# One graph layer with a gated unit in front of a plain graph layer: four queues put in another order, and the last subtraction of the blend given to TensorE

## The reference, cut to what matters

```
h = relu(layernorm(x))
conv = relu(bn2(conv1d_17(relu(bn1(conv1d_1(h.T))))) + h.T).T   # 17 taps along the nodes
s = h @ w_se.T + b_se                                            # 3 coordinates a node
A = exp(-|s_n - s_m|^2) * adj
nmp = A @ relu(h @ w_msg.T + b_msg)
r, z = sigmoid(gates of [conv, nmp] and h);  c = tanh(i_n + r * h_n)
x = x + (1 - z) * c + z * h
h2 = relu(layernorm(x))
x = x + adj @ (h2 @ weight) + bias
```

## Time and profile before

| | |
|---|---|
| median of 3 runs | 334.1 us (333.93 to 334.57) |
| the profiled execution | 334.82 us |
| its span, first to last instruction | 333.0 us |
| granted TensorE clock, mean | 1.000 |
| PE busy | 322.2 us, 97% of the span |
| PEld busy | 290.7 us, 87% |
| DVE busy | 259.7 us, 78% |
| ACT busy | 224.1 us, 67% |
| POOL busy | 145.3 us, 44% |

### The profile page before, as it was taken

One profiled execution on the slowest core, in us unless ns is written; L12 is line 12 of the kernel. 1 busy time (PEld: TensorE's weight loads), 2 busy tenths in 40 slices (PEclk: granted clock), 3 DMA queues, 4 the chain that ended last, 5 costly groups with the idle time before them and its releaser, 6 DMA issues.

```text
span 333.0 us, 6260 instructions
## 1 busy us (share of the span) xinstructions
PE 322.2 (97%) x2162; PEld 290.7 (87%) x2162; DVE 259.7 (78%) x746; ACT 224.1 (67%) x434; POOL 145.3 (44%) x128
## 2 busy tenths in 40 slices
PE   8799999989999999999999999999999999989995
PEld 5588787879889997899989998899989998889894
DVE  5788999899679977799679977789678766772475
ACT  2899668778668767687758776696767745443353
POOL 7130352139701793129801694119901594127014
PEclk9999999999999999999999999999999999999999
DMA  7902000002200131002300131001200010000003
GB/s 240 341 15 94 1 2 0 3 0 89 102 2 3 33 126 33 0 1 66 126 2 0 34 105 54 0 0 67 65 0 0 2 47 18 1 2 0 3 0 127
DMA packets 7951, 15.02 MB, mean 45 GB/s; under 512 B 1008, under 2 KB 1648, under 8 KB 7792
## 3 DMA queue, kind: packets, MB, share of 16 engines
q1 hardware_dynamic: 7776, 14.62, 12.9%
q10 hardware_dynamic: 144, 0.01, 0.0%
HBM read 10.43 MB, written 4.19 MB: 44 GB/s over the span
## 4 chain that ended last, share of the span: by engine, by line
issue 44%; POOL 30%; PE 11%; DVE 8%; ACT 4%; DMA 1%; POOLq 1%; DVEq 0%
POOL rs L1424 5%; POOL rs L1419 3%; POOL x_ring L1461 3%; POOL px L1010 3%; POOL px L1020 3%; POOL ac L1016 2%; POOL px L1013 2%; POOL base L1478 2%; POOL base L1469 2%; POOL base L1467 2%; POOL base L1475 2%; ACT hn L719 2%; DVE st L1033 1%; DMA x_ring<-x_in 1%; PE pP L328 1%
## 5 line engine op out<-in xcount | busy, mean ns | idle before, releaser
L1424 POOL TENSOR_TENSOR rs<-ve,neg_half 128x4 f32<-128x4 f32 x15 | 18.7, 1249 | 132.1 <-DVE ve L1192 132.1
L327 PE MATMUL pP<-cx_hi,conv_hi 128*128 128x256 f32 (+1 forms) x179 | 53.7, 300 | 0.0
L329 PE MATMUL pP<-cx_hi,conv_lo 128*128 128x256 f32 (+1 forms) x179 | 51.4, 287 | 0.0
L328 PE MATMUL pP<-cx_lo,conv_hi 128*128 128x256 f32 (+1 forms) x179 | 51.4, 287 | 0.0
L327 PE MATMUL pQ<-cx_hi,conv_hi 128*128 128x256 f32 (+1 forms) x139 | 41.6, 299 | 2.0 <-DVE cx_lo L1116 1.2
L329 PE MATMUL pQ<-cx_hi,conv_lo 128*128 128x256 f32 (+1 forms) x139 | 39.7, 285 | 0.0
L328 PE MATMUL pQ<-cx_lo,conv_hi 128*128 128x256 f32 (+1 forms) x139 | 39.6, 285 | 0.0
L327 PEld LDWEIGHTS pP<-cx_hi,conv_hi 128*128 128x128 f32 x179 | 33.9, 190 | 0.5
L328 PEld LDWEIGHTS pP<-cx_lo,conv_hi 128*128 128x128 f32 x179 | 33.8, 189 | 0.5
L329 PEld LDWEIGHTS pP<-cx_hi,conv_lo 128*128 128x128 f32 x179 | 33.7, 188 | 0.4
L327 PEld LDWEIGHTS pQ<-cx_hi,conv_hi 128*128 128x128 f32 x139 | 26.2, 189 | 2.6 <-issue 2.4
(11 more groups left out here) (281 smaller groups left out, 967.6 us busy)
## 6 DMA issues: line engine op xcount, KB each, us to landing
x_ring<-x_in SPq DMA_DIRECT2D x16, 256.0 KB, 2.8
adj_ring<-adj_in SPq DMA_DIRECT2D x16, 256.0 KB, 3.0
out<-x_ring SPq DMA_DIRECT2D x15, 256.0 KB, 2.0
work<-conv_in SPq DMA_DIRECT2D x1, 1088.0 KB, 7.7
x_ring<-gate_in SPq DMA_DIRECT2D x1, 576.0 KB, 8.3
out<-x_ring SPq DMA_DIRECT2D x2, 128.0 KB, 1.8
early<-early_in SPq DMA_DIRECT2D x1, 129.5 KB, 3.8
late<-late_in SPq DMA_DIRECT2D x1, 128.0 KB, 8.4
```

The source lines that it names most:

```text
L327: pe.matmul(acc, w_hi, m_hi, start=start, stop=False)
L328: pe.matmul(acc, w_hi, m_lo, start=False, stop=False)
L329: return pe.matmul(acc, w_lo, m_hi, start=False, stop=stop)
L1424: pool.tensor_tensor(rs2[g % 2][:], ve2[g % 2][:], neg_half[:, 0:GG], ALU.pow).then_inc(rs2_set, 1)
```

## The change

1. SP loads x of group 0 in two transfers of two graphs each, on a semaphore each; DVE's statistics of graphs 0 and 1 wait for the first, those of 2 and 3 for the second.
2. The order on ACT in the opening: `place_bias(0)` comes between `hidden_hi(0)` and `hidden_hi(1)`; `round_w(0)` ahead of `conv1_out(0)`; `hidden_graphs(0)` behind `conv1_out(1)`; `hidden_copy(0)` behind `split_hi_first(0)`; later `hidden_graphs(2)` ahead of `decay(0)`. On DVE `split_w(0)` comes ahead of `sum_odd` and `less_odd`.
3. The order on DVE in step 1: both `split_lo(1, 3)` and `split_lo(1, 4)` move back, `coordinates(4)` and `right_rows(4)` forward. In step 7, `between(7)` comes ahead of `shift2(13)`.
4. The blend of group 15: DVE no longer subtracts. PE multiplies `zh` by the identity (`last_turn_kept`) and adds `cand` times the negated identity to it (`last_turn_less`), in the same bank. POOL makes `neg_ident` once, in the opening.
5. PE in `ending()`: the three groups of `keep_clock` (2, 4 and 3 matmuls) go; `layer2(12)` and `layer2(13)` come behind the last turn; `end_pass(0)` comes ahead of `layer2(14)`. ACT makes the first half of group 15's h2 ahead of `turned_up(14)`. POOL does `with_bias(14)` ahead of `scale2_half(0)`, once DVE has made the last `cand`.

```diff
-            load_x(0)
+            sp.dma_start(two(xs(0), 0), two(x_in[:, 0:W], 0)).then_inc(x_first, 16)
+            sp.dma_start(two(xs(0), 1), two(x_in[:, 0:W], 1)).then_inc(x_loaded[0], 16)
...
+            def last_turn_kept():
+                have(pe, zh_set, END + 1)
+                have(pe, v_set, END + 1)
+                for j in range(GG):
+                    pe.matmul(graph(pI, j), lane(zh[END % 2], j), ident[:], start=j == 0, stop=True, skip_group_check=True)
+
+            def last_turn_less():
+                have(pe, zn_set, END + 1)
+                pe.wait_ge(neg_set, 1)
+                for j in range(GG):
+                    last = pe.matmul(graph(pI, j), lane(cand[END % 2], j), neg_ident[:], start=False, stop=True,
+                                     skip_group_check=True)
+                last.then_inc(o_placed, 1)
...
-                keep_clock(2)
+                last_turn_kept()
+                last_turn_less()
                 layer2(END - 3)
-                keep_clock(4)
-                o_turn(END)
                 layer2(END - 2)
                 adj_h2(END - 1)
+                end_pass(0)
                 layer2(END - 1)
-                keep_clock(3)
-                end_pass(0)
                 end_pass(1)
...
                 hidden_hi(0)
+                place_bias(0)
                 hidden_hi(1)
-                place_bias(0)
-                hidden_copy(0)
-                hidden_graphs(0)
+                act.wait_ge(conv_loaded, 16)
+                round_w(0)
                 conv1_out(0)
                 conv1_out(1)
-                act.wait_ge(conv_loaded, 16)
-                round_w(0)
+                hidden_graphs(0)
                 split_hi_first(0)
+                hidden_copy(0)
                 hidden_copy(1)
                 hidden_graphs(1)
                 round_w(1)
...
                 first(3)
+                hidden_graphs(2)
                 decay(0)
                 left_rows(1)
-                hidden_graphs(2)
...
                 second(END - 1)
-                turned_up(END - 1)
                 have(act, l1_done, END - 1)
                 for j in range(GG):
+                    if j == 2:
+                        turned_up(END - 1)
...
                 blend_start(qq)
+                shift2(pp)
                 if t == 1:
-                    split_lo(1, 3)
-                shift2(pp)
+                    coordinates(a)
                 blend_end(qq)
...
                     right_rows(a)
+                    if t == 1:
+                        split_lo(1, 3)
                     pairs(b)
+                    if t == 1:
+                        split_lo(1, 4)
+                if middle and not front:
+                    between(t)
                 shift2(qq)
...
                 blend_start(END)
                 shift2(p)
-                blend_end(END)
+                scaled_candidate(END)
                 residual(END)
...
+                pool.tensor_scalar(neg_ident[:], ident[:], -1.0, None, ALU.mult).then_inc(neg_set, 1)
...
                 scale2(END - 1)
+                pool.wait_ge(zn_set, END + 1)
+                with_bias(END - 1)
                 scale2_half(0)
```

More of the change, by code:

```diff
@@ L69, in gnn_kernel @@
         ident = sb("ident", [128, 128])
+        neg_ident = sb("neg_ident", [128, 128])
         warm = sb("warm", [128, 1])
@@ L152, in gnn_kernel @@
             sem, ("st1_set", "mv1_set", "ve1_set", "rs1_set", "nb1_set", "hn_set"))
-        hn_half = sem("hn_half")
+        hn_half, x_first, neg_set = sem("hn_half"), sem("x_first"), sem("neg_set")
         hT_placed, hhi_set, hG_set, hT_set, hlo_set = map(sem, ("hT_placed", "hhi_set", "hG_set", "hT_set", "hlo_set"))
@@ L1029, in normalise1 @@
                 lane = slice(lanes[0][2], lanes[-1][2] + 1)
-                for g in groups:
-                    dve.wait_ge(x_loaded[g % XRING], 16 * (g // XRING + 1))
+                if groups[0]:
+                    for g in groups:
+                        dve.wait_ge(x_loaded[g % XRING], 16 * (g // XRING + 1))
+                else:
+                    dve.wait_ge(x_first, 16)
                 for g, j, i in lanes:
+                    if (g, j) == (0, 2):
+                        dve.wait_ge(x_loaded[0], 16)
                     last = dve.bn_stats(st1[:, i, :], xs(g, j))
@@ L1165, in blend_start, with scaled_candidate, blend_end @@
                 dve.scalar_tensor_tensor(zh[g % 2], tz, 1.0, half(hT, g), ALU.add, ALU.mult).then_inc(zh_set, 1)
-            def blend_end(g):
+            def scaled_candidate(g):
                 have(dve, nn_set, g + 1)
                 dve.scalar_tensor_tensor(cand[g % 2], tz, 1.0, cand[g % 2], ALU.subtract, ALU.mult).then_inc(zn_set, 1)
+            def blend_end(g):
+                scaled_candidate(g)
                 have(dve, zn_set, g + 1)
@@ L1252, in opening @@
                 hidden_lo(1)
+                split_w(0)
                 sum_odd()
                 less_odd()
-                split_w(0)
                 split_lo_first(0)
@@ L1320, in step @@
                     hidden_lo(b)
-                    coordinates(a)
+                    if t > 1:
+                        coordinates(a)
                     pair_rows(a)
@@ L1324, in step @@
                 normalise2(qq)
-                if t == 1:
-                    split_lo(1, 4)
                 if front:
                     right_rows(a)
+                    if t == 1:
+                        split_lo(1, 3)
                     pairs(b)
+                    if t == 1:
+                        split_lo(1, 4)
+                if middle and not front:
+                    between(t)
                 shift2(qq)
@@ L1332, in step @@
                     masked(a)
-                if middle:
                     between(t)
@@ L1512, in ending @@
                 pool.wait_ge(nb2_set, END + 2)
-                with_bias(END - 1)
                 with_bias(END)
```

## The result

The changed kernel takes 339.02 us (338.7 to 339.06), the kernel before 334.34 on the same chip (333.93 to 334.71): a ratio of 1.0138, with a 95% interval of 1.0124 to 1.0153. The prediction was 332.5 us, with a range from 331.2 to 334.1. It was wrong in sign, and the range did not hold the time.

A forecast was written before the change was run, and what follows sets the result against it. PE was taken to bound the kernel, with its few waits in the opening, step 1, step 7 and the ending. The terms +0.8 - 0.85 - 1.0 - 0.5 = -1.55 us gave 332.5 us, range 331.2 to 334.1.

The forecast's parts named there:

- the price of the two matmul groups in the ending: Ending: last_turn_kept and last_turn_less were each to take 0.89 us, like a group of four full matmuls.
- the slack in step 1: Step 1: PE could come 0.88 us earlier before running up against DVE's xc_lo of the second half.
- the split of the first load: Opening: earlier statistics of graphs 0 and 1 end in ACT's wait for the bias; costed at nothing.
- the clock: Rival, chance 0.1: PE's opening holes of 1.4 and 1.3 us drop it to 1.2 GHz; 3 us gives 335.5.
- Step 7: between(7) ahead of shift2(13) removes PE's wait: -1.0 us, between 0.8 and 1.05.
- `hidden_graphs(2)`: Opening: its earlier copy on ACT removes PE's wait before the transposes of group 3: -0.5 us, between 0.4 and 0.6.
- The order of ACT in the opening: hidden_hi(1) behind place_bias(0) makes the first tap late, at 16.7: +1.3 us, between +0.8 and +1.7.
- Step 1: Moving two split_lo back on DVE shortens three waits of PE: -0.85 us, gain between 0.4 and 1.4.
- its lower bound: Step 1: gain only 0.4 us if POOL gets in front of shift2(1), making between(1) late by half of 1.25 us.
- The ending: New last turn and order: -0.5 us at the last sum, between nothing and -1.1; residual(15) 1.1 us earlier.
- What lies behind the residual: Ending: residual(15) starts at 322.5 and the last sum at 329.7, after delays through second(14), turned_up(14) and layer2(14).

The follow-up runs named there:

- fifth: Kernel before with only between(7) put ahead of shift2(13) on DVE; 333.54 us, ratio 0.9978.
- tenth: Kernel before with only between(7) ahead of shift2(13) and hidden_graphs(2) ahead of decay(0); 333.07 us, ratio 0.996.
- eleventh: Kernel before with between(7) ahead of shift2(13), hidden_graphs(2) ahead of decay(0), and the change's step 1 order with sums_lo(4) ahead of shift1; 332.78 us, ratio 0.9951.
- fourth kernel: Changed kernel with identity matmuls filling PE's two holes, between conv1(0) and conv1(1) and ahead of messages(0); 336.79 us, ratio 1.0061.
- ninth kernel: Kernel before with the change's DVE order in step 1, plus sums_lo(4) ahead of shift1 there; 334.17 us, ratio 0.9991.
- eighth kernel: Kernel before with the change's ending alone, zh and cand of group 15 written graph by graph; 334.4 us, ratio 0.9999.
- first kernel: Changed kernel with place_bias(0) back behind hidden_hi(1) on ACT; 335.9 us, ratio 1.0042.
- second kernel: Kernel before with only place_bias(0) put ahead of hidden_hi(1) on ACT; 335.43 us, ratio 1.0021.
- twelfth: Kernel before with the change's ending, zh and cand of group 15 written graph by graph, and layer2(12) ahead of the last turn; 335.92 us, ratio 1.0043.

## Why the prediction was wrong, step by step

Four terms failed: the price of the two matmul groups in the ending (0.89 us each, measured 1.94 and 1.86), the slack in step 1 (0.88 us, measured 0.15), the split of the first load (costed at nothing, measured 0.5), and the clock, which was left out of the sum (2.27 us in front of the first tap).

**Step 7: right.** -1.0 was forecast, and the traces have -1.01 in the change, -1.02 in the fifth and tenth kernels. `between(7)` takes 0.75 us beside POOL's sum, and `nb` behind it 0.72, as it still has to wait for POOL. That the one excludes POOL and the other not is what the Trainium skill says (SBUF — State Buffer, Who interferes with whom), and these rows agree. The prediction had read the agreement off, which don't show it: there `between(7)` begins 0.07 us before POOL's sum ends. In the kernel before, step 1 shows it: `between(1)` takes 0.74 us from 73.77, beside POOL's sum from 73.28 to 74.56.

**`hidden_graphs(2)`: right.** -0.5 was forecast. From the first tap to the transposes of group 3 the kernels without it need 13.57 us, or 12.95 where PE's wait of 0.6 us for `pair` (L1092 before) is absent; the tenth and eleventh, with it, need 12.28 and 12.99. That is -0.67 and -0.58. The -1.36 of the change in this stretch is this and the wait for `pair`, which is absent there, but for 0.1.

**The order of ACT in the opening: right in itself.** +1.3 was forecast, 1.09 measured (fourth kernel, with the clock whole), and the first tap's 16.7 with a bias at 10.0 answers to 6.49 behind the bias.

**The opening, two terms wrong.** First the split, costed at nothing with an upper bound of one issue, 0.43 us: alone it costs 0.5 us on the median. The prediction saw one bias write and took its 10.0 for a constant; the whole opening hangs on it (the first tap comes 5.38 to 5.40 us behind the write in all ten kernels with the old order on ACT there), and it scatters by 0.7 us. The means with and without the split are 0.8 us apart (10.96 and 10.14), so of the 1.18 in the trace of the change some is scatter. Why the load lands later with the split was not tested; the one more issue (every later one of SP comes 0.5 us later) is enough in size, but the scatter is of the same size. Second the clock: it was a rival with a chance of 0.1 and a price of 3 us. It happened, in all four executions, and costs 2.27 in front of the first tap (2.6 by the ratios of the change and the fourth kernel). The rival had holes of 1.4 and 1.3 us. The first was 2.33, as the bias came late, and the clock had fallen before the second began; whether it falls behind holes of the forecast's size no run shows. What weighed against the rival was only a granted clock of 1.00 in a window in which PE was busy for 2.77 of 4 us. In the change it was busy for 1.67 of 4 (0.76 and 0.91), and by the forecast's own times for little more than 1.5 (0.6 us to the end of `conv1(0)`, 1.0 for `conv1(1)`): the chance had to be worked out from the predicted timeline, not from the one before.

**Step 1: the sign was wrong.** -0.85 was forecast, with a lower bound of -0.4; +0.57 was measured, and +0.53 with nothing else changed. Two things failed. The slack that the forecast took from the earlier trace rows, 0.88 us, is not the smallest one. In the trace before there was this, 6 us earlier:

```profile
82.11 0.68 DVE L1112 TENSOR_TENSOR n_lo<-pF,n_hi 128x512 fp32r<-128x512 f32 x1
...
82.94 1.13 PE L447 MATMUL pF<-att,msg 128*128 128x128 f32 x8
```

DVE is through with pF at 82.79, and PE writes it from 82.94: 0.15 us of slack. It is no wait, so the view of the waits doesn't show it, and it is no input of the matmul but a bank that must be free. As long as DVE's results behind that point come when they did, PE gains 0.15 at most. (The ninth kernel took this one out of the way and won 0.11, as PE then waited for DVE's `att`.) The rest of the error is the case that the prediction named as its lower bound, POOL in front of `shift2(1)`. It came about through the moved instruction itself: `split_lo` (L1170, two SBUF inputs) now runs from 75.84 to 76.59 into POOL's start, POOL's sum takes 1.73 us instead of 1.28, and `nb` behind it 1.26 instead of 0.16. The lower bound had priced that with "half"; it ate the whole gain of DVE's queue: `n_lo` starts 20.90 us behind the first mark of the step, where it was 20.33. (`shift1`, 1.23 us beside POOL's next sum, was no shorter before, 1.24.)

**The ending: the sign was wrong.** -0.5 was forecast, +1.66 measured. The step that failed is the price of `last_turn_kept` and `last_turn_less`: the forecast took "a group of four full matmuls takes 0.89 us", from groups with a contiguous stationary operand. These read with a stride of four elements and take 1.94 and 1.86: +2.0 us, and `residual(15)` comes 1.0 us later instead of 1.1 earlier. `o_turn` reads with the same stride, and its weight loads were a warning that the prediction didn't look for: 0.204 and 0.210 us in the means of two groups of 32, where the transposes with a contiguous stationary operand (`x_turn`, L403) take 0.141 (two kinds of transpose in one trace; no run changes the stride of one alone). The Trainium skill speaks against the change here, and the prediction passed over it (SBUF — State Buffer, Door 1: The DMA port swizzle): SBUF has lines of 16 bytes, and an access that goes to a new line each time pays. Four fp32 elements are just one line, and the loads (0.33 against 0.19), DVE's scattered writes (1.07 against 0.68) and the transposes (0.21 against 0.14) agree. The same note gives four fp32 elements as how far one can stride for free; read as a stride of four, that doesn't agree with these rows.

What lies behind the residual was forecast well: 7.2 us from it to the last sum, measured 7.27, before 6.61. The eighth kernel, with contiguous operands, wins nothing (0.9999), but there DVE's scattered writes hold the residual at 4.30 us behind `adj_h2(12)`, where the forecast had 3.75. Without them the last sum would come some 0.5 us earlier, which is the forecast's gain; that is an estimate from these rows, and no run shows it. So what failed in the ending is the price of the products, and not the chain behind them.

Of the 0.66 us that the new order loses behind the residual, 0.60 is there when h2 is whole: 5.16 us behind the residual in the change (ACT is through at 332.48), 4.56 before. The rows say where: `turned_up(14)` runs for 0.60 us between the halves, from 331.12, while the inputs of the second half were ready at 330.97. No run took it out.

**The sum.** Bias 1.18, order of ACT 1.09, clock 2.27, the stretch behind it -1.36, step 1 +0.57, step 7 -1.01, ending +1.66: +4.40, against 4.36 at the last sum and 4.7 on the medians. By the single timed parts: 0.5 + 0.7 (first line alone) + 0.7 - 0.75 + 1.3 = 2.45, less the 0.6 of `hidden_graphs(2)`, and with the clock 2.27: 4.1. Of the rivals the one by the clock came true in that the clock fell, not in the two holes that were to bring it down; and without it the kernel would still have been slower, as the fourth kernel shows (1.0061).

## What to carry to other kernels

A slack taken for a bound must be the smallest one between the place of the gain and the end: for each bank that PE overwrites, look for who reads it last, as such a near miss is in no list of waits. A new matmul is priced by a row with the same precision and the same stride of its operands, not by its shape alone. When an edit opens a hole in PE's work, lay out PE's timeline as the edit will make it, and give the fall of the clock its chance from that: here it fell in every execution, and filling the holes won 2.3 us in front of the first tap. And look at the granted clock of every timed execution, not of the trace alone: in three kernels here it fell in some and held in others, and one trace shows only one of the two.

## What the runs showed of the hardware that was not expected

- Eight records of four full-fp32 matmuls with a stationary operand at a stride of four fp32 elements take 2.03 to 2.10 us, with weight loads of 0.33 us; the same data contiguous take 1.06 to 1.13 and 0.19. Transposes with that stride load in 0.21, contiguous ones in 0.14.
- A DVE instruction of two SBUF inputs and 512 elements takes 1.07 us when each element is written 128 places behind the one before, and 0.68 when they lie together.
- The clock fell to 0.50 behind one hole of PE: of 2.33 us in the change (at 13.7 us, 0.6 us after PE had begun again), of 2.75 in the first kernel (at 15.3, 1.0 us after). Behind one of 2.05 in the second kernel's trace it held. It was low for 6.8 us in the change and 3.4 in the first kernel.
- The same kernel can do both: the mean granted clock was 0.995 in two of seven executions of the first kernel, 0.994 or 0.995 in two of ten of the second and in six of twelve of the twelfth, and 0.998 to 1.000 in their others.
- The bias write, which needs one small load behind 1088 KB of another, begins between 9.78 and 10.50 us in kernels that don't differ there (ACT waited for the load in four of nine), and the whole opening moves with it. PE's wait of 0.6 us for `pair` in the opening is there in some of them and absent in others.
- The exclusion of DVE and POOL runs both ways: POOL's sum took 1.73 us instead of 1.28 behind a DVE instruction that had begun 0.2 us before it.
